# Three of four heads' probabilities turned in blocks through HBM, page copies in the first stage, a weight chunk an item

## The reference

```python
# 1: a projection with a low-rank adapter chosen per batch, then causal attention
y  = x @ W.T + bias + scale[id] * (x @ A[id].T) @ B[id].T
qkv = y @ w_qkv.T + b_qkv          # 32 query heads, 8 key/value heads of 16; rope on q and k
x1 = x + softmax(q k / 16, causal) v @ w_dense.T + b_dense
# 2: attention over a paged cache, 32 query heads, 8 key/value heads of 128
q, k, v = x1 @ Wq.T, x1 @ Wk.T, x1 @ Wv.T      # rms norm and rope on q and k
kc, vc = k_cache[block_table], v_cache[block_table]    # 16 pages of 32 tokens a batch
o = softmax(q [kc, k] * scale, masked by length) [vc, v]
h = o @ Wo.T
# 3: a linear layer with a low-rank part whose rank each token's gate chooses
out = x1 + h @ W.T + b + lora(h)
```

## Time and profile before

| | us |
|---|---|
| median of 3 runs | 1381.01 |
| lowest, highest | 1377.62, 1381.92 |
| the profiled execution | 1385.71 |
| its span in the profile | 1383.9 |

### The profile page before, as it was taken

How to read it: one execution, slowest core, us unless ns; L and a number is a source line. 1 busy time by engine, 2 the same in 40 slices (tenths; PEclk the granted TensorE clock), 3 DMA queues, 4 the chain that set the end, 5 groups by cost and what they waited for, 6 DMA issues and landing times. The chain is left out here.

```text
span 1383.9 us, 26262 instructions
## 1 busy us (share of the span) xinstructions
PE 1271.4 (92%) x7464; PEld 1072.3 (77%) x7464; DVE 990.4 (72%) x2388; ACT 833.0 (60%) x2501; POOL 824.0 (60%) x775
## 2 busy tenths in 40 slices
PE   6899998377699999999999999999999999999988
PEld 4667665266588888888888888888888888888878
DVE  3678776155477877787778777787878777878766
ACT  2667775253376666665766666575757666766641
POOL 0465565163376757665876676576758665876632
PEclk8899999689799999999999999999999999999999
DMA  8544544444545454555455455545454555455441
GB/s 280 159 154 147 167 146 136 138 123 127 156 110 143 120 152 124 140 122 152 114 140 146 129 132 131 148 115 146 115 153 119 144 128 159 113 136 143 123 141 62
DMA packets 288562, 191.49 MB, mean 138 GB/s; under 512 B 151201, under 2 KB 256674, under 8 KB 287266
## 3 DMA queue, kind: packets, MB, share of 16 engines
q1 hardware_dynamic: 287408, 189.64, 50.1%
q10 hardware_dynamic: 1010, 0.17, 0.1%
HBM read 143.60 MB, written 79.69 MB: 161 GB/s over the span
## 5 line engine op out<-in xcount | busy, mean ns | idle before, releaser
L1745 POOL TENSOR_TENSOR b_p_l<-b_moved,b_p_h 128x640 fp32r<-128x640 f32 x128 | 200.6, 1567 | 243.9 <-ACT b_p_h L1492 180.7
L1480 ACT ACTIVATE b_pf<-b_sm,b_mn 128x640 f32<-128x640 f32 x256 | 212.2, 829 | 140.0 <-DVE b_mn L1590 140.0
L1590 DVE CUSTOM_DVE_ANT_0 b_sm<-ps,mask_row,b_rstd 128x640 f32<-128x640 f32 x256 | 224.5, 877 | 46.4 <-PE ps L1267 42.0
L1492 ACT ACTIVATE b_p_h<-b_moved 128x640 fp32r<-128x640 f32 x128 | 94.6, 739 | 255.6 <-DMA b_moved<-blocks_of_probs 255.5
L1265 PE MATMUL ps<-b_kt_h,b_qt_h 128*128 128x320 f32 x512 | 172.0, 336 | 26.6 <-DVE b_mn L1590 23.3
L1626 DVE SCALAR_TENSOR_TENSOR b_hacc<-ps,b_ri,b_hacc 128x512 f32<-128x512 f32 x248 | 182.7, 737 | 4.6 <-PE ps L1267 4.3
L1265 PE MATMUL ps<-b_w_h,x1t_h 128*128 128x512 f32 (+1 forms) x512 | 180.2, 352 | 0.2
L1266 PE MATMUL ps<-b_w_l,x1t_h 128*128 128x512 f32 (+1 forms) x512 | 174.4, 341 | 0.0
L1267 PE MATMUL ps<-b_w_h,x1t_l 128*128 128x512 f32 (+1 forms) x512 | 174.2, 340 | 0.0
L1267 PE MATMUL ps<-b_kt_h,b_qt_l 128*128 128x320 f32 x512 | 160.2, 313 | 0.0
L1266 PE MATMUL ps<-b_kt_l,b_qt_h 128*128 128x320 f32 x512 | 160.2, 313 | 0.0
(11 more groups left out here) (170 smaller groups left out, 3410.9 us busy)
## 6 DMA issues: line engine op xcount, KB each, us to landing
blocks_of_probs<-b_blk SPq DMA_DIRECT2D x128, 320.0 KB, 2.6
b_moved<-blocks_of_probs SPq DMA_DIRECT2D x512, 80.0 KB, 2.1
kv_of_batch<-in_kv SPq DMA_DIRECT2D x128, 256.0 KB
b_ck<-kv_of_batch SPq DMA_DIRECT2D x64, 256.0 KB, 4.0
b_cv<-kv_of_batch SPq DMA_DIRECT2D x256, 64.0 KB, 2.0
raw<-in_w SPq DMA_DIRECT2D x32, 384.0 KB, 5.8
raw<-in_wo SPq DMA_DIRECT2D x32, 256.0 KB, 3.9
a_xt<-in_xt SPq DMA_DIRECT2D x8, 256.0 KB, 6.1
```

The lines of the kernel that those rows point to most:

```text
L1480: act.activation(pf[:, h % 2], sm[:, h % 2], ACT.Exp, bias=mn[:, m.b % 2, h:h + 1], scale=-1.0, accum_out=rs[:, m.b % 2, h:h + 1]).then_in ...
L1492: act.activation(blocks_of(p_h[:, :, h * P:(h + 1) * P]), moved[:, d].rearrange("p (a t j) -> p a t j", a=LT, j=QUAD), ACT.Copy).then_inc( ...
L1590: dve.tensor_tensor_reduce(sm[:, h % 2], score_row, mask_row[:, m.b], rstd[:, m.b % 4, h:h + 1], -MASKED, ALU.add, ALU.min, mn[:, m.b % 2, ...
L1745: pool.tensor_tensor(blocks_of(p_l[:, :, h * P:(h + 1) * P]), moved[:, d].rearrange("p (a t j) -> p a t j", a=LT, j=QUAD), blocks_of(p_h[: ...
```

## The change

- `BY_DMA` becomes heads 0, 1, 2 and `BY_PE` head 3. `blk` and `moved` keep two rooms, so head 2 shares that of head 0; waits are added for it. PE's `turn_probs(m, 2)` goes. DVE turns the blocks of head 2 behind `minima(m, 3)`, where `low(m, 2)` stood later. SP sends head 2 away and back behind head 1's return, ahead of `value_rows`. `high_moved(m, 2)` and `low_moved(m, 2)` stand in the slot after, on ACT ahead of `exponent(m, 1)`, on POOL between `rms` and `rope_keys`; `high_moved(m, 0)` goes behind `exponent(m, 3)`.
- All 128 pages are copied in the slots -1 to 6, 16 in each, a batch a slot with its own semaphore. Page numbers are loaded four at a time. The second stage copies none.
- Weights come a chunk an item: 384 KB chunks at b = 2, 3, 4, 5, 256 KB chunks at b = 6, 7 and two at b = 0.
- The sum of keys' rope goes from DVE to POOL (behind `normalize(b, 3)`), and `with_bias` goes behind `normalize(b, 5)`.

```diff
-BY_DMA = (0, 1)
-BY_PE = (2, 3)
+BY_DMA = (0, 1, 2)
+BY_PE = (3,)
+ROOMS = 2
...
-def gather(sp, t, pages, kv_dram, gathered, n):
-
-    page = sp.value_load(pages[0:1, n:n + 1], min_val=0, max_val=PAGES - 1)
-    sp.dma_start(kv_dram[n // NPP, :, n % NPP], t["kv"][bass.ds(page, 1)].rearrange("a g n -> (a g) n")).then_inc(gathered, 16)
+def gather_four(nc, sp, t, pages, kv_dram, gathered, first):
+
+    _, four = nc.values_load_multi_w_load_instructions(pages[0:1, first:first + FOUR], engines=(mybir.EngineType.SP,),
+                                                       min_val=0, max_val=PAGES - 1)
+    for k in range(FOUR):
+        n = first + k
+        sp.dma_start(kv_dram[n // NPP, :, n % NPP], t["kv"][bass.ds(four[k], 1)].rearrange("a g n -> (a g) n")).then_inc(gathered, 16)
...
-                    for n in range((b + 1) * EARLY, (b + 2) * EARLY):
-                        gather(sp, t, pages, kv_dram, gathered, n)
-                if b >= LAST:
-                    first = EARLY * B + TAIL * (b - LAST)
-                    for n in range(first, first + TAIL):
-                        gather(sp, t, pages, kv_dram, gathered, n)
+                    for n in range((b + 1) * NPP, (b + 2) * NPP, FOUR):
+                        gather_four(nc, sp, t, pages, kv_dram, gathered[b + 1], n)
...
-                dve.tensor_tensor(kr[:], rope_a[:, H1:].unsqueeze(2).broadcast_to(shape),
-                                  rope_b[:, H1:].unsqueeze(2).broadcast_to(shape), ALU.add).then_inc(rope_done, 1)
...
+            def rope_keys(a):
+                if a == 0:
+                    pool.wait_ge(rope_first, 1)
+                pool.wait_ge(rope_ab, a + 1)
+                wait(pool, kt_ps, a)
+                shape = [P, G1, 4, D1]
+                pool.tensor_tensor(kr[:], rope_a[:, H1:].unsqueeze(2).broadcast_to(shape),
+                                   rope_b[:, H1:].unsqueeze(2).broadcast_to(shape), ALU.add).then_inc(rope_keys_done, 1)
...
 def key_rows(m):
+                if m.g == 0:
+                    sp.wait_ge(gathered[m.b], 16 * NPP)
...
 def blocks_back(m, h):
-                wait(sp, ml_sb, len(BY_DMA) * (m.n - 1) + d + 1)
+                wait(sp, ml_sb, len(BY_DMA) * m.n + d + 1 - ROOMS if d >= ROOMS else len(BY_DMA) * (m.n - 1) + last_in_room(d) + 1)
...
 SP, slot(m, one, two, last):
                 blocks_back(m, 1)
+                blocks_away(m, 2)
+                blocks_back(m, 2)
                 if two:
                     value_rows(two)
-                if m and m.b == 3:
-                    for c in range(KT):
-                        chunk(m.g + 1, c)
-                if m and m.b == 7 and one:
-                    for c in range(KT, 2 * KT):
-                        chunk(m.g + 1, c)
+                if m.b in (2, 3, 4, 5):
+                    chunk(m.g + 1, m.b - 2)
+                if m.b in (6, 7) and m.g + 1 < G:
+                    chunk(m.g + 1, KT + m.b - 6)
+                if m.b == 0 and m.g > 0:
+                    chunk(m.g, KT + 2)
+                    chunk(m.g, KT + 3)
...
 PE, slot:
-                turn_probs(m, 2)
...
 ACT, slot:
                 if last:
                     high(last, 3)
+                    high_moved(last, 2)
                 exponent(m, 1)
...
-                high_moved(m, 0)
                 if last:
                     output(last)
                 exponent(m, 3)
-                high(m, 2)
+                high_moved(m, 0)
...
 DVE, turn_blocks(m, h):
-                wait(dve, blk_out[d], 16 * m.n)
-                dve.transpose(by_quadrant(blk[:, d]), by_tile(pf[:, h % 2])).then_inc(blk_sb, 1)
+                wait(dve, blk_out[d - ROOMS], 16 * (m.n + 1)) if d >= ROOMS else wait(dve, blk_out[last_in_room(d)], 16 * m.n)
+                dve.transpose(by_quadrant(blk[:, d % ROOMS]), by_tile(pf[:, h % 2])).then_inc(blk_sb, 1)
 DVE, slot:
                 minima(m, 3)
+                turn_blocks(m, 2)
                 if last:
                     output(last)
                     invert(last)
-                low(m, 2)
...
 POOL, slot:
                 if one:
                     rms(one)
+                if last:
+                    low_moved(last, 2)
+                if one:
                     rope_keys(one)
```

More of the change, by code:

```diff
@@ L44 @@
 EPS = 1e-6
[L45 to L47 removed]
+FOUR = 4
 LAST = B - 1
[L49 to L50 removed]
+BY_DMA = (0, 1, 2)
+BY_PE = (3,)
+ROOMS = 2
 QUAD = 32
@@ L557, in rope_sum @@
                 dve.wait_ge(rope_ab, a + 1)
[L558 removed]
                 wait(dve, qt_ps, a)
                 dve.tensor_tensor(qr[:], rope_a[:, 0:H1].rearrange("p h d -> p (h d)"),
[L561 to L564 removed]
+                                  rope_b[:, 0:H1].rearrange("p h d -> p (h d)"), ALU.add).then_inc(rope_done, 1)
             def keys_out(a):
@@ L690, in rope @@
                 wait(pool, rope_done, a)
+                wait(pool, rope_keys_done, a)
                 qk = qkv[:, 0:NQK * D1].rearrange("p (h d) -> p h d", d=D1)
@@ L732, in slot @@
                     normalize(b, 3)
+                if inside(b + 1):
+                    rope_keys(b + 1)
                 if b == LAST - 1:
                     next_q_weights(0, range(0, 1))
-                if inside(b):
-                    with_bias(b)
                 if b == LAST:
@@ L743, in slot @@
                     normalize(b, 5)
+                    with_bias(b)
                 if b == LAST:
@@ L1118, in phase2 @@
         hacc = sb("hacc", [P, B, D])
-        blk = sb("blk", [P, len(BY_DMA), NK])
-        moved = sb("moved", [P, len(BY_DMA), NK])
+        blk = sb("blk", [P, ROOMS, NK])
+        moved = sb("moved", [P, ROOMS, NK])
         const_sb = sem("const_sb")
@@ L1167, in phase2, with last_in_room @@
         blocks_dram = nc.dram_tensor("blocks_of_probs", [len(BY_DMA), P, NK], F32).ap()
+        def last_in_room(d):
+            return max(e for e in range(len(BY_DMA)) if e % ROOMS == d % ROOMS)
         def by_quadrant(ap):
@@ L1227, in slot @@
                     blocks_away(m, 1)
-                if two and two.g == 0 and two.b == 6:
-                    sp.wait_ge(gathered, 16 * NPP * B)
                 if two:
@@ L1491, in high_moved @@
                 wait(act, pvh_ps, m.n)
-                act.activation(blocks_of(p_h[:, :, h * P:(h + 1) * P]), moved[:, d].rearrange("p (a t j) -> p a t j", a=LT, j=QUAD),
+                act.activation(blocks_of(p_h[:, :, h * P:(h + 1) * P]), moved[:, d % ROOMS].rearrange("p (a t j) -> p a t j", a=LT, j=QUAD),
                                ACT.Copy).then_inc(mh_sb, 1)
@@ L1549, in _ @@
             high(end, 3)
+            high_moved(end, 2)
             h_out(act, 2)
@@ L1744, in low_moved @@
                 wait(pool, pv_ps, m.n)
-                pool.tensor_tensor(blocks_of(p_l[:, :, h * P:(h + 1) * P]), moved[:, d].rearrange("p (a t j) -> p a t j", a=LT, j=QUAD),
+                pool.tensor_tensor(blocks_of(p_l[:, :, h * P:(h + 1) * P]), moved[:, d % ROOMS].rearrange("p (a t j) -> p a t j", a=LT, j=QUAD),
                                    blocks_of(p_h[:, :, h * P:(h + 1) * P]), ALU.subtract).then_inc(ml_sb, 1)
@@ L1776, in _ @@
             slots(pool, slot)
+            low_moved(end, 2)
             pool_ffn(pool)
@@ L1787, in build_program @@
         pages = sb("pages", [1, B * NPP], I32)
-        gathered = ctx.enter_context(nc.semaphore("gathered"))
+        gathered = [ctx.enter_context(nc.semaphore(f"gathered{b}")) for b in range(B)]
         raw_in = [ctx.enter_context(nc.semaphore(f"raw_in{c}")) for c in range(KT)]
```

9 lines of the change are left out of this document (4 added, 5 removed).

## The result

| | before | after |
|---|---|---|
| median of 4 runs each, us | 1379.89 | 1417.61 |
| lowest, highest | 1377.62, 1381.92 | 1412.51, 1418.39 |
| profiled execution, its span | 1385.71, 1383.9 | 1416.97, 1415.2 |

The changed kernel is slower: after over before is 1.0266 (95% interval 1.0236 to 1.0296). Predicted were 1333 us and "faster" with a chance of 0.86; the time lies above the range.

What follows compares the result with a forecast made beforehand. It took PE as today's bound and SP's queue as the next: 14.5 + 0.6 + 0.5 + 0.6 = 16.2 us an item. The sum -36 - 15 + 0 + 3 = -48 us gave span 1335.5, median 1333, range 1290 to 1378.

Steps and rivals of the forecast that it cites:

- SP becomes the bound of the second stage: SP's queue, second stage: its round of 16.2 us an item would exceed PE's 15.2 us.
- A single chunk can hide part of its transfer in its latency; I take 0.6 us, between 0 and 1.15: SP's queue, weight chunk directly ahead of head 0's blocks: delays them 0.6 us an item, between 0 and 1.15.
- the change of stages: Between the stages: without eight copies ahead, the last x1 store issues earlier, gaining 15 us (13.7 to 17.2).
- the first stage: First stage, PE near full: result 0 (-3 to +3); 16 copies fit the 25.00 us slot if one load serves four.
- the second rival: SP between a block's departure and return: round trips get so long it is slower, from 16.98 us on; chance 0.11.
- PE's transposes: PE, second stage: five transposes fewer save 0.47 us an item, 30 us alone, leaving PE's item at 15.2 us.
- SP's slack today: SP's queue in the kernel before: 10.1 us of 15.66 an item is used, the rest is slack.
- the third rival: SP binds the first stage: loading four page numbers costs like four loads, 8 us more a slot, 1373; chance 0.08.
- The sign "PE waiting for `p_h` of `moved`": PE, second stage: would wait there ahead of `values_of_highs`, with items 16.2 us apart, nearly even.
- The shared room costs nothing more: Room of `moved` shared by heads 0 and 2: head 0 is free at about 884, as head 2's return starts.
- GpSimd, "nothing of it is late by itself": GpSimd, second stage: gains a `low_moved` of 1.57 us, busy 8.81 becomes 10.4 of about 16 us, without lateness.
- the last rival: POOL and ACT bind: `low_moved` of head 2 makes the next keys late, about 16.9 us an item, 1376; chance 0.06.

Runs made afterwards that it cites:

- the two-heads run: The changed kernel with its third head (head 2) turned by PE again, two heads through HBM; 1305.31 us, ratio 0.9439 to the kernel before.
- the two runs whose rounds are 17.01 and 17.04: Changed kernel with weight chunks issued by ScalarE (1382.90 us); changed kernel with chunk behind head 0's departure and value rows behind head 2's (1383.88 us).
- the run with small chunks: The changed kernel with each weight chunk cut to an eighth of its columns, usable for timing only; 1372.15 us, ratio 0.9904 to the kernel before.
- the copies alone: The kernel before with only the page copies all moved into the first stage; 1335.41 us, ratio 0.9647.
- the chunk in the wait: The changed kernel with the weight chunk issued behind head 0's departure instead of ahead of it; 1374.15 us, ratio 0.9925 to the kernel before.
- the other queue: The changed kernel with weight chunks issued by ScalarE at the end of its slot instead of by SP; 1382.90 us, ratio 1.0002 to the kernel before.
- third buffer: The changed kernel with weight chunks issued by ScalarE, plus a third buffer for turned blocks; 1359.61 us, ratio 0.9807 to the kernel before.

## Why the prediction was wrong, step by step

The mechanism was right in the main: "SP becomes the bound of the second stage", shown by SP's waits and by the two-heads run. What failed is the size of the round, and in it above all the term **"A single chunk can hide part of its transfer in its latency; I take 0.6 us, between 0 and 1.15"**. It measured 1.28 in the mean and 1.80 behind a chunk of 384 KB, beyond its upper end. That end was a burst's delay over four: 4.28 us in the mean (6.48 against 2.20). But the four are issued over 1.85 us, in which the first can already move, so each shows less of itself than a single one does. That reason is argued; the numbers are measured. For it speaks that chunks 2.0 to 2.9 us ahead leave head 0 at 2.29 us in the two-heads run, against 4.12 with a chunk 0.53 us ahead here.

Term by term, us an item:

| | predicted | measured |
|---|---|---|
| trips of heads 0, 1, 2 without a chunk | 2.21 + 2.62 + 2.62 = 7.45 | 2.35 + 2.75 + 2.70 = 7.80 |
| three ways back, value rows, with long issues | 7.08 + 0.6 = 7.68 | 5.48 + 1.95 = 7.43 |
| chunk's issue | 0.47 | 0.42 |
| chunk's delay of head 0 | 0.6 | 1.28 |
| wait for `kt_l` before the key rows | not counted | 0.30 |
| gaps between issues, short waits for `low_moved` | partly in the above | 0.3 |
| **round** | **16.2** | **17.5** |

The two are 1.3 us apart: 0.7 by the chunk, 0.35 by the trips, 0.3 by the keys' wait (2.4 us in the item of b = 6; before, it stood in the queue's spare time), 0.3 by gaps, less 0.3. Over 62 items that is 82 us. The forecast span was 1335.5 and the measured one 1415.2, 79.7 us apart; the change of stages with the first stage (3.7 better than forecast) and the end (0.7 worse) make the rest. The threshold of the second rival, 16.98 us, held: 17.53 is beyond it, and the two runs whose rounds are 17.01 and 17.04 have the ratio 1.0002. Its chance of 0.11 was too small for a threshold 0.8 us above the sum, where the extras taken into it were themselves uncertain by more.

The chunk is the largest miss and not the whole of it. With hardly any chunk the prediction's own sum gives 15.6 us; the run with small chunks has 16.75, and 1372 us as its median. So 1333 was out of reach even had the 0.6 been right.

- *PE's transposes* (0.47 us, item 15.2): right, undisturbed items are 15.12 us apart. Worth nothing where SP sets the item.
- *SP's slack today*: right; it went to 0.
- *The change of stages* (15 us, 13.7 to 17.2): 17.2 by the copies alone; the 18.7 at item 1 contain 1.2 of the first stage.
- *First stage* (0; load for four at the price of one): the load was right, 0.80 us, and the third rival falls. The slot became shorter, 24.3 instead of 25.0 us, with the rope sum and the bias moved. The prediction saw nothing to win there; the last x1 came 1.2 us earlier.
- *The end* (+3): +3.7.
- *The sign "PE waiting for `p_h` of `moved`"*: wrong. That wait is 3.1 us over 393:1345; PE stops for the queries' rope behind GpSimd, 64.1 us. Nor are the items nearly even: from item 1 on they are 15.1 to 22.0 us apart.
- *"The shared room costs nothing more"*: right in the changed kernel, where all waits beyond the landings are 0.20 us an item. But it looked only at head 0 making room for head 2. The wait that shows once the chunk is out of the way is the other one, head 0's way back for head 2 of the item before (0.55 us with the chunk in the wait, 0.79 with the other queue).
- *GpSimd, "nothing of it is late by itself"*, and the last rival (16.9 us by POOL and ACT): in the changed kernel GpSimd is hidden by the queue. But relieved of the chunk the round stops at 16.75 (small chunks), 17.0 (other queue) and 16.7 (third buffer), with waits for GpSimd in it each time: two bounds nearly level, where the prediction had one. How GpSimd's three waits (buffer, `kt_l`, `v_l`) share in that was not separated.

## What to carry to other kernels

A queue that issues and then waits for a landing counts as an engine: add up its issues and landings per item before giving it another round trip, and when the sum is as near to the break-even as here (16.2 to 16.98 us), treat the sign as open. Bulk loads spread one an item cost nothing in a queue with spare time (here they gained 2% over bursts) and most of their delay in one without (0.80 of 1.28 us). A burst's delay divided by its members is not an upper end for one of them.

## Seen of the hardware, not expected

- A chunk of 384 KB issued 0.53 us ahead of a 320 KB transfer delays its landing by 1.80 us, one of 256 KB by 1.06, two of 256 KB by 0.97, each against the same chunk cut to an eighth; four of 384 KB by 4.28 (kernel before, against 2.20).
- On the same queue a chunk 2.0 to 2.9 us ahead leaves the landing at 2.29 us (two heads).
- Another engine's queue does not take the delay away: with the chunk 1.91 us ahead the landing took 3.2 us, against 2.33 with over 4 us.
- Loading four page numbers into registers with one instruction took 0.80 us, one 0.73.
